# Taylor-attention and gated FFN block on one core: x transposed by the load, scaled and split on GpSimd, its norms sent through DRAM

## What is computed

```python
normed = gamma * (x / norm(x)) * 128 ** 0.5
q, k, v = heads(normed @ w_q) * 16 ** -0.5, heads(normed @ w_kv)
q, k = taylor2(q), taylor2(k)           # 1, x, all products x_i x_j / sqrt(2)
out = (q @ (k.T @ v)) / max(q @ sum(k), 1e-5)
x1 = layernorm(x + out @ w_out)
h = silu(x1 @ w1) * (x1 @ w2); h = gelu(h @ h1); h = gelu(h @ h2)
y = layernorm(x1 + h @ w3)              # ternary weights with scales
```

## Time and profile before

| | |
|---|---|
| median of 3 runs | 569.73 us (567.96 to 570.62) |
| the profiled execution: time, span | 568.82 us, 567.0 us |
| granted TensorE clock, mean | 0.983 |
| PE matmul busy | 541.8 us, 96% of the span |
| PE weight load busy | 408.8 us, 72% |
| DVE busy | 457.4 us, 81% |
| ACT busy | 460.6 us, 81% |
| POOL busy | 159.1 us, 28% |
| chain that ended last | PE 88%, issue 4%, DVE 2%, ACT 1% |
| DMA | 12.25 MB, mean 22 GB/s |

### The profile page before, as it was taken

The page is one execution under the profiler, slowest core; times in us unless marked ns, Lnnn a source line. Parts: engine busy times, 40 slices in busy tenths (PEclk is TensorE's granted clock), DMA queues, the critical chain, the costliest instruction groups (busy, mean ns, idle before and its releaser), DMA issues.

```text
span 567.0 us, 11454 instructions
## 1 busy us (share of the span) xinstructions
PE 541.8 (96%) x3598; PEld 408.8 (72%) x3598; DVE 457.4 (81%) x981; ACT 460.6 (81%) x952; POOL 159.1 (28%) x246
## 2 busy tenths in 40 slices
PE   7839999999999999999999999999999999999994
PEld 4426787778688786868878686877878687786772
DVE  4865769878797987879798787979888787968764
ACT  4757798897979888897988889797988979787773
POOL 3541323133142322315141231514223141400000
PEclk9977999999999999999999999999999999999997
DMA  8000000000000000000000000000000000000000
GB/s 285 5 22 1 5 17 1 20 20 20 21 13 24 0 18 18 18 18 18 18 0 18 18 18 18 18 18 0 18 18 18 18 18 18 1 18 1 20 1 37
DMA packets 7366, 12.25 MB, mean 22 GB/s; under 512 B 816, under 2 KB 1840, under 8 KB 7344
## 3 DMA queue, kind: packets, MB, share of 16 engines
q1 hardware_dynamic: 7056, 11.86, 6.4%
q10 hardware_dynamic: 288, 0.10, 0.1%
HBM read 7.77 MB, written 4.19 MB: 21 GB/s over the span
## 4 chain that ended last, share of the span: by engine, by line
PE 88%; issue 4%; DVE 2%; ACT 1%; POOLq 0%; POOL 0%; DVEq 0%
PE fps L422 27%; PE fps L425 27%; PE ring L359 6%; PE ring L389 5%; PE ring L339 5%; PE ring L313 4%; PE ring L398 3%; PE ring L406 3%; PE ring L320 2%; PE fps L467 1%; PE fps L414 1%; PE ring L346 1%; PE ring L300 1%; PE ring L369 1%; DVE h L910 1%
## 5 line engine op out<-in xcount | busy, mean ns | idle before, releaser
L422 PE MATMUL fps<-hid_hi,w_hi 128*128 128x512 f32 x576 | 229.6, 399 | 0.0
L425 PE MATMUL fps<-hid_lo,w_hi 128*128 128x512 f32 x576 | 227.1, 394 | 1.3 <-DVE hid_lo L924 0.9
L697 ACT ACTIVATE hid_hi<-fps,col 128x512 fp32r<-128x512 f32 x128 | 90.2, 705 | 54.5 <-PE fps L425 54.5
L425 PEld LDWEIGHTS fps<-hid_lo,w_hi 128*128 128x128 f32 x576 | 108.3, 188 | 25.7 <-DVE hid_lo L924 2.5
L422 PEld LDWEIGHTS fps<-hid_hi,w_hi 128*128 128x128 f32 x576 | 108.4, 188 | 25.0 <-issue 3.4
L924 DVE TENSOR_TENSOR hid_lo<-fps,hid_hi 128x512 fp32r<-128x512 f32 x128 | 88.1, 689 | 31.5 <-ACT fps L699 30.1
L699 ACT ACTIVATE fps<-fps,col 128x512 f32<-128x512 f32 x128 | 86.5, 675 | 0.0
L648 ACT ACTIVATE phiT<-ring 128x512 f32<-128x512 f32 x127 | 77.1, 637 | 3.7 <-PE ring L339 2.6
L910 DVE SCALAR_TENSOR_TENSOR h<-fps,col,gate_zo 128x512 f32<-128x512 f32 x64 | 47.8, 748 | 39.4 <-ACT gate_zo L684 33.8
L249 DVE TENSOR_TENSOR phi_k<-phi_k 128x896 f32<-128x896 f32 x64 | 69.2, 1085 | 1.4 <-ACT v_one L621 1.3
L339 PE MATMUL ring<-qT,sel 128*128 128x512 f32 x128 | 53.1, 420 | 6.2 <-DVE qT L833 3.6
(11 more groups left out here) (99 smaller groups left out, 899.2 us busy)
## 6 DMA issues: line engine op xcount, KB each, us to landing
x_b<-in_x SPq DMA_DIRECT2D x16, 256.0 KB, 2.7
out<-gate_zo SPq DMA_DIRECT2D x16, 256.0 KB, 2.0
w_raw<-in_h SPq DMA_DIRECT2D x2, 1024.0 KB, 9.0
w_raw<-in_w SPq DMA_DIRECT2D x3, 256.0 KB, 4.1
sel_raw<-in_sel SPq DMA_DIRECT2D x1, 320.0 KB, 5.3
w_qkv_raw<-in_w_kv SPq DMA_DIRECT2D x1, 128.0 KB, 2.8
const<-in_consts ACTq DMA_DIRECT2D x1, 92.0 KB, 3.1
w_qkv_raw<-in_w_q SPq DMA_DIRECT2D x1, 64.0 KB, 3.6
```

The lines of the kernel that those rows point to most:

```text
L422: nc.tensor.matmul(fps[:, bank, :], w[:, o:o + P], hi, start=start, stop=False)
L425: return nc.tensor.matmul(fps[:, bank, :], w[:, o:o + P], lo, start=False, stop=stop)
L697: nc.scalar.activation(hid[1 - layer][0][:, m, :], fps[:, bank, :], ACT.Gelu, scale=scale)\
```

## The change

The host gives a second copy of `x` with features first, `xT` (16 x 128 x 512, tokens in natural order). For each batch from 1 on, this is loaded as `x_cols`. POOL multiplies it by a row of norms, `rn_row`, twice (into the rounded `xnT_hi` and into `x_scaled`) and subtracts for `xnT_lo`. The norms are still made with tokens on partitions, from a load of their own (`x_nrm`); `rn` is stored to 512 words in DRAM and loaded back to all partitions. This norm is made half a step ahead, so `square` and `sum_squares` of batch `t+1` are earlier in the lists. The residual is a third load (`x_res`). Batch 0 goes by PE as before. Since tokens are in natural order in `att` now, `project_out` takes every fourth column of it as weights. The fill is written anew: four parts of weights and six sums of their low bits, `sums_of_q` 0 to 2 and `rest_of_q` 0 of batch 1 behind the branch, `normed_cols(1)` ahead of `spread_rest(1)`, and `k_small(1, 1)` behind x1.

```diff
         WN = oh2 + KT * HID
-        LOADS = (3, 1, 1)
-        w_parts = ((0, oh1), (oh1, oh2), (oh2, WN))
+        LOADS = (2, 1, 1, 1)
+        w_parts = ((0, o3), (o3, oh1), (oh1, oh2), (oh2, WN))
+        half = KT * HID // 2
+        CHECKS = ((0, o3, 0), (o3, oh1, 1), (oh1, oh1 + half, 2), (oh1 + half, oh2, 2), (oh2, oh2 + half, 3),
+                  (oh2 + half, WN, 3))
         w_hi = sb("w_hi", [P, WN], F32R)
...
+            def load_norm_parts(n):
+                sp.wait_ge(sq_ready, n)
+                sp.dma_start(x_nrm[:, :, :], x_d[bass.ds(n, 1)].rearrange("b p j d -> (b p) j d"))\
+                    .then_inc(nrm_loaded, 16)
+            def load_cols(n):
+                if is_positive(n - 1):
+                    sp.wait_ge(x_scaled_ready, n - 1)
+                sp.dma_start(x_cols[:, :], xT[bass.ds(n, 1)].rearrange("b d n -> (b d) n")).then_inc(cols_loaded, 16)
+            def spread_norms(n):
+                sp.wait_ge(rn_ready, n + 1)
+                sp.dma_start(rn_d, rn[:, :]).then_inc(rn_stored, 16)
+                sp.wait_ge(rn_stored, 16 * n)
+                sp.dma_start(rn_row[:, :], rn_all).then_inc(rn_row_loaded, 16)
+            def load_residual(n):
+                if is_positive(n):
+                    sp.wait_ge(ring_free[bank_of(RING, "out")], read(RING, n, "out"))
+                sp.dma_start(x_res[:, :, :], x_d[bass.ds(n, 1)].rearrange("b p j d -> (b p) j d"))\
+                    .then_inc(res_loaded, 16)
...
             def step(t, par, front, middle, ffn, tail):
                 if front and not is_step(t, B - 1):
-                    if middle:
-                        sp.wait_ge(ring_free[bank_of(RING, "out")], read(RING, t, "out"))
-                    sp.dma_start(x_b[1 - par][:, :, :],
-                                 x_d[bass.ds(t + 1, 1)].rearrange("b p j d -> (b p) j d")
-                                 ).then_inc(x_loaded[1 - par], 16)
+                    if not is_step(t, 1):
+                        load_norm_parts(t + 1)
+                    load_cols(t + 1)
+                    spread_norms(t + 1)
+                if front:
+                    load_residual(t)
                 if tail:
                     sp.wait_ge(out_ready, t - 2)
                     sp.dma_start(out_d[bass.ds(t - 3, 1)].rearrange("b p j d -> (b p) j d"), o_b[:, :, :])\
...
-            load_ffn_weights(0, (o1, w1t), (o2, w2t), (o3, w3t))
+            load_ffn_weights(0, (o1, w1t), (o2, w2t))
+            load_ffn_weights(1, (o3, w3t))
             sp.dma_start(sel_raw[:, :], sel_d).then_inc(sel_loaded, 16)
-            peeled(step, 0)
-            load_ffn_weights(1, (oh1, h1t))
-            load_ffn_weights(2, (oh2, h2t))
+            sp.dma_start(o_b[:, :, :], x_d[1]).then_inc(x1_nrm_loaded, 16)
+            load_cols(1)
+            load_ffn_weights(2, (oh1, h1t))
+            load_residual(0)
+            spread_norms(1)
+            load_ffn_weights(3, (oh2, h2t))
             sp.dma_start(w_o[:, :], w_out).then_inc(w_out_loaded, 16)
+            sp.wait_ge(xn_ready, 1)
+            sp.dma_start(x_nrm[:, :, :], x_d[2]).then_inc(nrm_loaded, 16)
...
             def project_kv(t, j):
                 if j == 0:
-                    pe.wait_ge(ring_free[bank_of(RING, "xT")], read(RING, t, "xT"))
+                    pe.wait_ge(x_lo_ready, t + 1)
...
             def project_out(t):
                 pe.wait_ge(att_ready, t)
                 bank_wait(RING, ring_free, t, "out")
+                by_tile = att[:, :].rearrange("c (p j) -> c j p", j=NT)
                 for j in range(NT):
-                    mm = nc.tensor.matmul(ring[:, bank_of(RING, "out"), j * P:(j + 1) * P],
-                                          att[:, j * P:(j + 1) * P], w_o[:, :], start=True, stop=True)
+                    mm = nc.tensor.matmul(ring[:, bank_of(RING, "out"), j * P:(j + 1) * P], by_tile[:, j, :],
+                                          w_o[:, :], start=True, stop=True)
                 mm.then_inc(ring_full, 1)
...
             def steps_with(in_full):
                 def step(t, par, front, middle, ffn, tail):
                     if is_step(t, 2):
-                        for part in range(3):
+                        for part in range(4):
                             pe.wait_ge(w_hi_ready[part], 1)
+                        transpose_x1(1, 0)
+                        sums_of_q(1, 0)
                     if ffn:
                         layer1(t, 0, in_full)
                     if is_step(t, 2):
-                        sums_of_q(1, 3)
-                        sums_of_q(1, 4)
+                        sums_of_q(1, 1)
+                        rest_of_q(1, 0)
                     if ffn:
                         layer1(t, 1, in_full)
                     if is_step(t, 2):
+                        for f in (2, 3, 4):
+                            sums_of_q(1, f)
                         rest_of_q(1, 1)
                         sums_of_q(1, 5)
                         sums_of_q(1, 6)
...
-                    if front:
-                        transpose_x(t)
+                    if is_step(t, 0):
+                        transpose_x0()
...
             def second_step():
                 transpose_state(1)
                 transpose_rest(1)
-                transpose_x(1)
                 apply_main(1)
                 apply_rest(1)
...
                 project_out(1)
-                sums_of_q(1, 0)
-                sums_of_q(1, 1)
-                rest_of_q(1, 0)
-                pe.wait_ge(lo_sums_ready, 3)
-                nc.tensor.matmul(fps[0:1, 3, 0:3], half_c, lo_sums[:, :], start=True, stop=True)\
+                pe.wait_ge(lo_sums_ready, len(CHECKS))
+                nc.tensor.matmul(fps[0:1, 3, 0:len(CHECKS)], half_c, lo_sums[:, :], start=True, stop=True)\
                     .then_inc(lo_sums_added, 1)
-                sums_of_q(1, 2)
...
                 if middle:
                     ring_copy(t, "stateT", w_main[:, :], ring[:, bank_of(RING, "stateT"), 0:2 * P], half_c)
                     ring_copy(t, "restT", w_rest[:, :], ring[:, bank_of(RING, "restT"), 0:P])
-                if front:
-                    x_hi(t)
                 if is_step(t, 0):
+                    x0_hi()
+                    square(1)
...
                 if is_step(t, 1):
-                    weights_low_bits(1, 0)
+                    weights_low_bits(3)
+                    weights_low_bits(4)
...
                 if front:
                     copy_kv(t, 3)
                 if is_step(t, 1):
-                    weights_low_bits(2, 1)
+                    weights_low_bits(5)
+                if front and not is_step(t, 0) and not is_step(t, 1) and not is_step(t, B - 1):
+                    square(t + 1)
...
                 if is_step(t, 1):
-                    weights_low_bits(0, 2)
+                    square(2)
...
-                if front and not is_step(t, B - 1):
-                    square(t + 1, 1 - par)
...
                     gate_mult(t, 0)
                     gate_mult(t, 1)
-                if front:
-                    x_lo(t)
                 if ffn:
                     gate_lo(t, 0)
                     gate_mult(t, 2)
...
                     normalise(t)
                 if tail:
                     sum_z(t, 1 - par)
+                if front and not is_step(t, B - 1):
+                    sum_squares(t + 1)
                 if ffn:
...
                     x1_lo(t)
-                if front and not is_step(t, B - 1):
-                    sum_squares(t + 1)
...
             def first_step():
-                x_lo(0)
+                x0_lo()
+                sum_squares(1)
...
-            def normed_x(t, par):
+            def norm_of_x(t):
                 pool.wait_ge(ssc_ready, t + 1)
...
+            def normed_cols(t):
+                pool.wait_ge(cols_loaded, 16 * t)
+                pool.wait_ge(rn_row_loaded, 16 * t)
+                pool.wait_ge(ring_full, written(RING, t - 1, "qT"))
+                nc.gpsimd.tensor_tensor(xnT_hi[:, :], x_cols[:, :], rn_row[:, :], ALU.mult).then_inc(x_hi_ready, 1)
+                nc.gpsimd.tensor_tensor(x_scaled[:, :], x_cols[:, :], rn_row[:, :], ALU.mult).then_inc(x_scaled_ready, 1)
+                pool.wait_ge(x_scaled_ready, t)
+                pool.wait_ge(x_hi_ready, t + 1)
+                nc.gpsimd.tensor_tensor(xnT_lo[:, :], x_scaled[:, :], xnT_hi[:, :].bitcast(F32), ALU.subtract)\
+                    .then_inc(x_lo_ready, 1)
...
             def step(t, par, front, middle, ffn, tail):
                 if middle:
                     spread_rest(t)
+                if front and not is_step(t, 0):
+                    normed_cols(t)
                 if front:
                     k_small(t, 0)
+                if is_step(t, 0):
+                    norm_of_x(1)
                 if tail:
                     inv_std(t - 3, zveps_ready, zveps, zrstd, zrstd_ready)
```

(31 more changed lines are left out.)

114 lines of the change are left out of this document (68 added, 46 removed).

## The result

The changed kernel takes 588.1 us (median of 4 runs, 587.35 to 588.45), against 570.0 for the kernel before (4 runs, 567.96 to 570.62): a ratio of 1.0326, 95% interval 1.0304 to 1.0348. It is slower, as forecast, but by 18 us instead of 4, outside the range of 565.8 to 579. Its profiled execution has a span of 586.6 us at a mean granted clock of 0.978.

The account below looks back on a forecast made before the run. TensorE was taken to bound the 32.78 us period, with a loop through ScalarE and VectorE 0.35 us behind. 3.7 - 0.7 + 1.1 = +4.1 us on 568.82 gives 572.9; with 0.9 for the median, 573.8, range 565.8 to 579.

Parts of the forecast that it names:

- the term for the weights of `project_out`: TensorE's weight loads from words 16 bytes apart: taken as 0, upper bound +0.8 us in each step.
- the second meeting: VectorE's `normalise` multiply against GpSimd's `k_mid`: its 0.15 us wait was to shrink to about 0.05.
- the fill: Start of the kernel, where `normed_cols(1)` delays `spread_rest(1)` and step 1: +1.1 us, bounds -1 to +3.
- the first meeting: VectorE's `gate_lo` of tile 0 waits for GpSimd's `xnT_lo` pass: 0.7 us, bounds 0 and 1.0.
- Step 1: TensorE loses four transposes of `x` in each of the steps 2 to 15: 0.36 us less.
- Steps 2 and 3: ScalarE loses `x_hi`, VectorE's `gate_lo` starts 0.86 us earlier; `sum_squares` enters VectorE's serial stretch, 0.92 us later behind it.
- Step 4: GpSimd's three 128x512 passes behind `spread_rest`: 1.25 us each with two full operands, bounds 1.04 and 1.5; hidden from TensorE.
- Step 5: GpSimd's passes hold up VectorE: 0.7 us at `gate_lo`, while 0.15 at `normalise` shrinks to about 0.05.
- The first rival: GpSimd's passes take 1.04 us and miss VectorE at `gate_lo` and `normalise`: faster, 566.1 us, chance 0.27.
- VectorE's loop: Loop TensorE, ScalarE, VectorE, TensorE with 0.35 us slack; TensorE then waits for tile 3's operand, period +0.31 us.
- the third rival: Strided weight loads in `project_out` are slow, adding 0.8 us to TensorE: period +0.44, 577.8 us, chance 0.15.
- The steady sum: Period change in steps 3 to 14: -0.36 + 0.56 + 0.11 = +0.31 us, 12 times, +3.7 us.

Follow-up runs that it names:

- e6: e1 without the GpSimd pass that writes `x_scaled` (low part taken from `x_cols` directly): 567.3 us, ratio 0.9951 to the kernel before.
- e9: e1 with the three GpSimd passes moved to the end of the step before, waiting for VectorE's last `phi_k` products: 569.7 us, ratio 1.0019 to the kernel before.
- e1: The changed kernel with contiguous weights in `project_out`, residual and result going by tiles of 128 consecutive tokens: 584.5 us, ratio 1.0265 to the kernel before.
- e2: The kernel before, with only `project_out` reading its weights 16 bytes apart: 582.3 us, ratio 1.0233 to the kernel before.
- e3: The changed kernel with batch 0 loaded by tiles of consecutive tokens and `spread_rest(1)` ahead of `normed_cols(1)` on GpSimd: 583.9 us.

## Why the prediction was wrong

The step that failed first of all is the term for the weights of `project_out`, which was put at 0 and measures +0.85 us in every step. Two more failed: the second meeting, and the size of the fill. The direction, slower, was forecast from the first meeting and the fill, and both are there; but most of the 18 us has other sources than the forecast's 4. Step by step:

- **Step 1 (TensorE -0.36):** right. Without stride and meeting the distance is 32.33 to 32.34 (e6, e9), 0.44 less than before; 0.36 of it was forecast.
- **Steps 2 and 3 (`gate_lo` 0.86 earlier, `sum_squares` 0.92 later):** right. In e6 `gate_lo` starts 3.85 us behind the last product of layer 4, and 4.72 before: 0.87 earlier. `gelu_tile` starts 1.02 us behind `zveps`, and 0.17 before: 0.85 later.
- **Step 4 (a pass of 1.25 us):** 1.29 to 1.30 measured, 1.25 forecast.
- **Step 5, the meetings:** the first was right in place and size (0.7 us forecast, 0.70 to 0.82 measured). The second failed in every other step. "The 0.15 us at `normalise` shrinks to about 0.05" looked at the multiply alone. The row that decides is `den`, ahead of it, which I had not looked at:

```profile
125.67 0.19 DVE L848 TENSOR_SCALAR den<-wide 128x32 f32<-128x32 f32 x1
```

This is the row before. By the forecast's own shifts (VectorE 0.16 us earlier, TensorE and with it `k_mid` 0.36) `den` comes at 125.51 and `k_mid` at 125.59, 0.08 us apart; they are 0.06 apart in the short steps and in the other order by 0.03 in the long ones. When `den` loses, it waits, and the multiply too: 1.0 us together. The first rival named this knife edge ("less than 0.1 us decides") but priced it at 0.6.
- **VectorE's loop alone:** with one meeting and no stride I had 32.78 + 0.31 = 33.09; e1's short distance is 32.90. The mechanism is right, TensorE waits for the `lo` of tile 3, but the term is too high, +0.31 where +0.12 is measured. That the short distance of the changed kernel, 33.23, lies near the 33.1 of the forecast is luck: it is TensorE's own time with the stride, with no such wait. The 0.06 us in the forecast's ready time came without a source; the rows show it (VectorE done at 248.35, the load at 248.41).
- **"A stride is free there, and I take 0":** the failed step that weighs most, +0.85 in every step. The row of `den` was the wrong neighbour, on another engine and too short: at the 0.7 ns a word that the stride costs VectorE elsewhere (last section) its 28 further words would cost 0.02 us, just what they were seen to cost in all. The upper bound, +0.8 and twice the pair's time, is what was measured (0.207 us a pair against 0.101), and the third rival's mechanism is true; its sum took 0.8 us for the two `project_out` of the fill, where its own price gives 1.6. The sentence from the Trainium skill (Advanced Engine Details and Errata, section SBUF Cachelines) spoke against the change, and e2 agrees with it, with 324 against 191 ns.
- **The steady sum:** the third rival said that the stride and VectorE's loop don't add, +0.44 a step. They don't, and its 33.22 is the short distance, measured 33.23; but with the second meeting the larger one has 34.1, and the mean of 33.67 is +0.89.
- **The fill, "+1.1, bounds -1 to +3":** +5.8. I had the order on GpSimd but counted four things too low: the row's way through DRAM (7.2 us, not 4 to 5.4), the stride in batch 0 (0.86 us, last section), the stride in `project_out(1)` (2.10 us where it took 1.13), and that TensorE, left idle, does `apply` at a lower clock (+1.3). The last is seen in every run that keeps this order: at least 3.7 us idle and 3.16 to 3.64 us for `apply`. With the order of e3 it is under 0.5 us and 1.92. What each adds to the 5.8 was not measured apart. The gain from the earlier sum of the low bits did not come: the sum waits on VectorE behind `normalise(1)` and `sum_x1(1)`, which are late themselves.

## What to carry over

Price a stride by a row that reads as many words in the same way, and if there is none, let the upper bound have a rival of its own. Where GpSimd gets work, lay its rows beside VectorE's rows that read SBUF only, small ones too: what starts first wins, a wait can decide the next meeting, and the gap that costs nothing is one where VectorE reads PSUM or rests. Two losses under one period hide each other: take away both before judging either.
